# Second layer's causal attention: the output map applied to the values before mixing, one accumulation for all groups

## What is computed

```python
x = x + _L1_attn_ref(_layernorm(x), ...)

def _L1_attn_ref(x, ...):
    q, k, v = split(x @ c_attn_w.T + c_attn_b)      # 3 x 128 features
    q, k, v = heads(q), heads(k), heads(v)          # 16 heads of 8
    q_lat = q @ q2l_w.T + q2l_b                     # 8 -> 32
    k_lat = k @ kv2l_w.T + kv2l_b
    v_lat = v @ kv2l_w.T + kv2l_b
    q_lat = q_lat * cos + _rotate_half(q_lat) * sin
    k_lat = k_lat * cos + _rotate_half(k_lat) * sin
    q_for_k = q_lat @ wqk_w.T + wqk_b
    att = softmax(causal(q_for_k @ k_lat.T * 32 ** -0.5))
    y_lat = att @ v_lat                             # 32 wide
    y = y_lat @ l2o_w.T + l2o_b                     # 32 -> 8, the output map
    return merge(y) @ cproj_w.T + cproj_b
```

## Time and profile before

| | us |
|---|---|
| Median of 3 runs | 4223.95 (4214.59 to 4225.65) |
| The profiled execution's own time | 4192.95 |
| Its span | 4191.1 |
| PE busy / DVE busy / ACT busy / POOL busy | 3748.0 / 2446.0 / 1525.1 / 829.2 |

### The profile page before, as it was taken

One profiled execution on the slowest core, in us unless ns is written; L12 is line 12 of the kernel. 1 busy time (PEld: TensorE's weight loads), 2 busy tenths in 40 slices (PEclk: granted clock), 3 DMA queues, 4 the chain that ended last, 5 costly groups with the idle time before them and its releaser, 6 DMA issues. The chain is left out here.

```text
span 4191.1 us, 95747 instructions
## 1 busy us (share of the span) xinstructions
PE 3748.0 (89%) x38732; PEld 2389.5 (57%) x38732; DVE 2446.0 (58%) x6058; ACT 1525.1 (36%) x3430; POOL 829.2 (20%) x1464
## 2 busy tenths in 40 slices
PE   6998999988898889999979989999788988899999
PEld 3886885433354436665548868854333544366655
DVE  5767675565535466555466777656555344765554
ACT  4445443222222235532244454432222222354322
POOL 1441541010000104220024424400110001033200
PEclk9999999999999999999989999999989999999999
DMA  2000000100000000010010000001000000000100
GB/s 93 3 3 1 3 3 12 41 12 1 21 1 20 1 1 25 1 40 25 5 34 3 3 1 3 3 12 52 1 1 21 1 20 2 12 14 1 40 29 6
DMA packets 8680, 60.05 MB, mean 14 GB/s; under 512 B 893, under 2 KB 5297, under 8 KB 5937
## 3 DMA queue, kind: packets, MB, share of 16 engines
q1 hardware_dynamic: 8240, 53.90, 3.4%
HBM read 52.85 MB, written 1.05 MB: 13 GB/s over the span
## 5 line engine op out<-in xcount | busy, mean ns | idle before, releaser
L97 PE MATMUL psum<-ident_bf 128*128 128x512 bf16 x1528 | 399.3, 393 | 71.6 <-DVE l_attn_peak L930 54.7
L3106 ACT ACTIVATE l_attn_ax<-psum 128x128 f32<-128x128 f32 (+1 forms) x768 | 186.7, 279 | 394.2 <-PE psum L2921 274.8
L3345 DVE TENSOR_TENSOR l_attn_xx<-l_attn_xx,psum 128x256 f32<-128x256 f32 x512 | 205.3, 420 | 209.0 <-PE psum L2940 197.5
L438 ACT ACTIVATE l_ffn_silu<-psum 128x512 f32<-128x512 f32 (+2 forms) x208 | 124.2, 597 | 465.6 <-PE psum L404 411.2
L97 PEld LDWEIGHTS psum<-ident_bf 128*128 128x128 bf16 x1528 | 147.6, 102 | 250.0 <-DVE l_attn_peak L930 69.3
L503 DVE TENSOR_TENSOR l_ffn_hidden<-l_ffn_silu,psum 128x512 f32<-128x512 f32 (+2 forms) x176 | 120.5, 687 | 282.5 <-ACT l_ffn_silu L438 282.4
L103 PEld LDWEIGHTS psum<-streamed_weights,l_ffn_hidden 128*128 128x128 f32 (+2 forms) x1664 | 215.7, 192 | 121.2 <-issue 110.5
L2936 PE MATMUL psum<-l_attn_ax,l_attn_xx 64*64 64x64 f32 x5120 | 269.9, 225 | 0.0
L2940 PE MATMUL psum<-l_attn_xx,l_attn_ax 64*64 64x64 f32 x5120 | 261.9, 221 | 0.0
L3232 POOL TENSOR_TENSOR l_attn_part<-l_attn_ab,streamed_weights 128x128 f32<-128x128 f32 x640 | 245.8, 416 | 39.4 <-PE psum L2921 20.3
L930 DVE TENSOR_REDUCE l_attn_peak<-psum 128x4 f32<-128x2048 f32 (+3 forms) x128 | 186.5, 1488 | 99.4 <-PE psum L822 98.7
(11 more groups left out here) (535 smaller groups left out, 7843.4 us busy)
## 6 DMA issues: line engine op xcount, KB each, us to landing
streamed_weights<-pack_l_ffn SPq DMA_DIRECT2D x2, 5284.0 KB, 15.3
streamed_weights<-pack_l_attn SPq DMA_DIRECT2D x3, 2848.5 KB, 10.2
streamed_weights<-pack_l_ffn SPq DMA_DIRECT2D x2, 3972.0 KB, 12.7
streamed_weights<-pack_l_xattn SPq DMA_DIRECT2D x2, 2496.0 KB, 10.0
streamed_weights<-pack_l_ffn SPq DMA_DIRECT2D x2, 2192.0 KB, 8.3
streamed_weights<-pack_l_xattn SPq DMA_DIRECT2D x2, 2048.0 KB, 7.7
streamed_weights<-pack_l_ffn SPq DMA_DIRECT2D x2, 1923.0 KB, 7.9
streamed_weights<-pack_l_attn SPq DMA_DIRECT2D x2, 1107.5 KB, 5.2
```

The lines of the kernel that those rows point to most:

```text
L97: pe.matmul(self.bank(bank), self.ident_bf[:, :], self.ident_bf[:, :].unsqueeze(1).to_broadcast([P, NT, P]), start=True, stop=True)
L3106: act.activation(ax[b, p, :, :], m.psum[b, p, 0:P].rearrange("p (i t) -> p i t", i=2), ACT.Copy).then_inc(ax_ready, 1)
L3345: dve.tensor_tensor(both, both, m.psum[:, p, P:384], ALU.subtract).then_inc(x_less, 1)
```

## The change

The output map has 8 outputs for every head and is linear, and the softmax weights of a row sum to one, so `att @ v_lat @ l2o.T + b` can be had by mixing values that already went through the map, bias included. The change does that in the preparing block and then calls `causal_attention` as the third layer does.

- The values are made by group, transposed (128 rows of four heads' latents by 512 positions), at n = 1 (two) and n = 3 (two). ScalarE evicts them (`v_latent`).
- At n = 6 four products of 32 columns each apply the output map, into the four quarters of bank 1. ScalarE evicts them with the bias behind its last latent (`vT`); at n = 8 TensorE turns `vT` in four transposes, and ScalarE copies the result into the zeroed, spread-out `v` in four pieces. GpSimd zeroes `v` at the block's start. VectorE's four additions at the end are gone.
- `mixed` has one group, the division is done once, and `early` and the closing block's product and eviction are gone. `cproj`'s rows are reordered on the host.

```diff
-        mixed = sb("mixed", [P, G, T])
+        mixed = sb("mixed", [P, 1, T])
...
+            @block.gpsimd
+            def _(pool):
+                pool.memset(v[:, :, :, :], 0.0).then_inc(v_cleared, 1)
...
-                def values(pe, t):
-                    pe.matmul(m.bank(t), qkv[:, 2, t * P:(t + 1) * P],
-                              w["kv2l"].rearrange("p g c -> p (g c)"), start=True,
-                              stop=True).then_inc(v_psum, 1)
+                def values(g):
+                    if g == 3:
+                        pe.wait_ge(v_latent_ready, 1)
+                    pe.matmul(m.bank(g % 3), w["kv2l"][:, g, :], qkv[:, 2, :], start=True, stop=True).then_inc(v_psum, 1)
...
-                        values(pe, 0)
-                        values(pe, 1)
-                    if n == 2 * G - 1:
-                        values(pe, 2)
+                        values(0)
+                        values(1)
+                    if n == 3:
+                        values(2)
+                        values(3)
+                    if n == 6:
+                        pe.wait_ge(v_latent_ready, G)
+                        for g in range(G):
+                            rows = slice(32 * g, 32 * g + 32)
+                            ins = pe.matmul(m.psum[rows, 1, :], w["l2o"][:, g, rows], v_latent[:, g, :], start=True,
+                                            stop=True, skip_group_check=True)
+                        ins.then_inc(v_out_psum, 1)
                     if n == 2 * G:
-                        values(pe, 3)
+                        pe.wait_ge(vT_ready, 1)
+                        for t in range(NT):
+                            ins = pe.transpose(m.psum[:, 2, t * P:(t + 1) * P], vT[:, t * P:(t + 1) * P], m.ident)
+                        ins.then_inc(v_turned, 1)
...
+                    if 1 <= n <= G:
+                        act.wait_ge(v_psum, n)
+                        act.activation(v_latent[:, n - 1, :], m.bank((n - 1) % 3), ACT.Identity,
+                                       bias=w["kv2l_b"]).then_inc(v_latent_ready, 1)
+                    if n == 2 * G - 1:
+                        act.wait_ge(v_out_psum, 1)
+                        act.activation(vT[:, :], m.bank(1), ACT.Identity, bias=w["l2o_b"]).then_inc(vT_ready, 1)
+                act.wait_ge(v_turned, 1)
+                act.wait_ge(v_cleared, 1)
+                for g in range(G):
+                    act.activation(v[:, :, G * g:G * g + G, HD * g:HD * g + HD],
+                                   m.bank(2).rearrange("p (t q r d) -> p t q r d", t=NT, q=G, d=HD)[:, :, g, :, :], ACT.Copy)
...
-                            tmp = mixed[:, n - G, :]
+                            tmp = turned_k[:, n % 2, :]
...
-                for t in range(NT):
-                    dve.wait_ge(v_psum, t + 1)
-                    dve.tensor_tensor(v[:, t, :, :], m.bank(t).rearrange("p (h l) -> p h l", l=32),
-                                      w["v_b"].unsqueeze(1).to_broadcast([P, H, 32]), ALU.add)
...
-        def early(pe):
-            for g in range(G - 1):
-                pe.matmul(m.bank(0), w["l2o"][:, g, :], mixed[:, g, :], start=g == 0, stop=False)
...
-                         lambda g: m.const["ones"][:, 0:32], False, mixed, early)
+                         lambda g: m.const["ones_of"][:, g, :], True, mixed)
...
-                pe.matmul(m.bank(0), w["l2o"][:, G - 1, :], mixed[:, G - 1, :], start=False, stop=True).then_inc(y_psum, 1)
-                pe.wait_ge(y_ready, 1)
-                m.project(pe, q[:, 0, :], w["cproj"])
-
-            @block.scalar
-            def _(act):
-                act.wait_ge(y_psum, 1)
-                act.activation(q[:, 0, :], m.bank(0), ACT.Identity, bias=w["l2o_b"]).then_inc(y_ready, 1)
+                m.project(pe, mixed[:, 0, :], w["cproj"])
```

More of the change, by code:

```diff
@@ L978, in stage_l1_attn @@
         qkv = psb("qkv", [P, 3, T])
+        v_latent = psb("v_latent", [P, G, T])
+        vT = psb("vT", [P, T])
+        turned_k = psb("turned_k", [P, 2, T])
         LAT, ROT_BANKS = 3, (5, 7)
@@ L990, in stage_l1_attn @@
         v_psum = sem("v_psum")
+        v_latent_ready = sem("v_latent")
+        v_out_psum = sem("v_out_psum")
+        vT_ready = sem("vT")
+        v_turned = sem("v_turned")
+        v_cleared = sem("v_cleared")
         chain_sem = sem("pre_chain")
@@ L1071, in _ @@
                                           ALU.add, ALU.mult).then_inc(wqk_read, 1)
-                for t in range(NT):
-                    dve.wait_ge(v_psum, t + 1)
-                    dve.tensor_tensor(v[:, t, :, :], m.bank(t).rearrange("p (h l) -> p h l", l=32),
-                                      w["v_b"].unsqueeze(1).to_broadcast([P, H, 32]), ALU.add)
         pre.close()
-        def early(pe):
-            for g in range(G - 1):
-                pe.matmul(m.bank(0), w["l2o"][:, g, :], mixed[:, g, :], start=g == 0, stop=False)
         causal_attention(m, name, lambda g: q[:, g, :], lambda g: k[:, g, :], lambda g, r: 4 * g + r, v,
-                         lambda g: m.const["ones"][:, 0:32], False, mixed, early)
-        y_psum = sem("y_psum")
-        y_ready = sem("y_ready")
+                         lambda g: m.const["ones_of"][:, g, :], True, mixed)
         with nc.Block(no_gpsimd_drain=True) as block:
@@ L3780, in pack_l1_attn @@
             ("q2l_b", col(g("q2l_b"), 4)), ("kv2l_b", col(g("kv2l_b"), 4)),
-            ("v_b", np.broadcast_to(g("kv2l_b")[None], (P, 32))), ("wqk", wqk), ("wqk_b", col(g("wqk_b"), 4)),
-            ("l2o", l2o), ("l2o_b", col(g("l2o_b"), 16)), ("cproj", g("cproj_w").T)]
+            ("wqk", wqk), ("wqk_b", col(g("wqk_b"), 4)),
+            ("l2o", l2o), ("l2o_b", col(g("l2o_b"), 16)), ("cproj", g("cproj_w").T.reshape(4, 4, 8, P).transpose(1, 0, 2, 3).reshape(P, P))]
 def pack_l2_attn(i, const):
```

## The result

| | before | changed |
|---|---|---|
| Median of 6 runs each | 4224.17 us (4214.59 to 4225.65) | 4181.95 us (4171.18 to 4194.26) |
| Ratio to before, 95% interval | | 0.9905 (0.9885 to 0.9925) |
| Profiled execution, span | 4191.1 us | 4176.6 us |
| Mean granted clock of the profiled execution | 0.960 | 0.959 |

The two profiled executions, at nearly the same mean clock, are 14.5 us apart. Why the medians say 42 and the profiles 14.5 is what the experiments are about.

A forecast was written before the change was run, and what follows sets the result against it. It took TensorE and VectorE, chained between rotations, to bound the preparing block and exponentials the middle. Stage ends 14.5 us plus preparing blocks 1.0 made 15.5 us off 4223.95: 4208.4 us, range 4195 to 4219.

The forecast's parts named there:

- The end of the stage: Last exponential to projection: without waits for banks and division, output map and eviction, 3.63 us less a stage, 14.5 in four.
- the 30.5 forecast: Preparing block: the scores start 30.5 us after the stage's start, saving 0.5 us per pass, 1.0 in all.
- rival 2: Preparing block grows: the four map products run one after another, 2.7 us more a stage, 4219 us; chance 0.12.
- the change of shape: Output map at n = 6: switching TensorE's tiling twice costs 0.24 us a stage, 1 us in all.
- I count no gain: Pause before the scores, about 2.8 us: no protection against TensorE's clock falling, so no gain counted.
- the 0 of the middle: Mixing in pieces of at most 256 columns costs and saves 0, since the unchanged exponentials set the pace.
- signs of being wrong: Map products in sequence, VectorE waiting for the last rotation, changed exponentials' pace, or first reduction 1.5 us after scores start.
- Rival 1: Clock holds at the scores: stretches match the third layer's, 24.0 us less, 25 us in all, 4199 us; chance 0.14.
- Rival 3: Lower clock falls into worse places: each changed stage loses 1 us more, gain 11.5 us, 4212 us; chance 0.10.
- Rival 4: Slower: new preparing-block waits at n = 6 and n = 8 lower the clock, +57 us net, 4281 us; chance 0.04.

The follow-up runs named there:

- with the pause: Changed kernel with four idle VectorE additions at the preparing block's end, making TensorE's pause before the scores 6.02 us: 4202.77 us, 0.9986 of the kernel before.
- Three shifts: Kernel before with idle VectorE memsets ahead of each pass's first layer, about 1, 2 or 3 us a pass: 4195.48, 4199.18 and 4198.34 us.
- shift 3: Both kernels with the longest idle VectorE memsets ahead of each pass's first layer, 6 us added in all: before 4198.34 us, changed 4197.25 us.
- first comparison: Kernel before and changed kernel, neither with added idle work, six runs each: 4224.17 and 4181.95 us, ratio 0.9905.

## Why the prediction was wrong

**Right in the structure.** The end of the stage is 8.36 us, 3.63 less, in all four. The block is 30.48 us for the 30.5 forecast; VectorE's idle time is 1.99 before the third rotation and 1.10 before the sixth, as forecast; the transposes are done at 975.65, before VectorE's seventh rotation ends at 977.08 (976.39 + 0.69). The map's four products hold the next back by 1.00 us (970.65 to 971.65), so rival 2 is refuted, and the change of shape costs 0.11 rather than 0.24 us above the 0.89 of the earlier trace rows. At the same clock the whole gives 15.9 us.

The Trainium skill, page "TensorEngine Tiling (Array Packing)", section "Key Properties", says that a change of tiling mode drains TensorE; the trace leaves about a tenth of a microsecond for that in the block.

**The step that failed** is "I count no gain" in the part on the clock, together with the 0 of the middle: both treated the clock's losses as a part of the kernel that stays. The 0 rested on the exponentials setting the pace; at the lower level TensorE sets it (the 3.12 us for which an exponential waits above). Two of the prediction's own signs of being wrong came: a first reduction 1.55 us after the scores start, and another pace of the exponentials in a group. The level does not hold through the scores, as predicted, but the conclusion did not follow. The fall came 1.5 us into the scores instead of in the pause, and what counts as much, a later one no longer met the first mixings. In the profiles of before and after that is 26.6 − 14.5 = 12.1 us of the second-layer stretches; of these 6.5 us lie between the first and fourth exponential (from 10.93, 10.93, 10.94 and 10.91 to 9.30 in each stage), 5.6 before the first.

**The medians.** Before's 4224.17 us is a span of about 4222. No clock is on record for these six runs; by the line it was near 0.9496 (0.957 − (4222.3 − 4201.0) / 2880); the changed kernel's six runs have 4180.2 and 0.9583. By this estimate the clock makes 0.0087 x 2880 = 25 us of the 42, structure the other 17. That the mean clock of the changed kernel is higher is measured; that it is so for a reason of the change is shown only for the second-layer stages at this position (with the pause the loss comes back). Three shifts give the kernel before a clock of 0.959 to 0.960 too, and shift 3 takes it from the changed one. So the 27 us beyond the forecast are not the change's own: with 1 to 3 us of idle work a pass the difference was 16.1, 14.8 and 1.1 us. The prediction subtracted from a median that lay high in its own scatter, in the three runs then known as in the first comparison, and its range held only 10 to 13 us for the clock; 4190 to 4224 in unchanged code says it needed twice that.

**The rivals.** Rival 1 had nearly the right size for the stretches, 24.0 us for 26.6 measured (its total, 4199, is 17 us above the time), by luck: the clock did not hold through the scores, and where it was made to, the changed kernel's stages did not gain. The Trainium skill, page "TensorE: Matmul & The Clock Gate", section "Why this matters for your kernels", advises against long idle gaps; the traces agree that the 3.01 us pause itself stays at 1.00 and 6.02 us do not, but the fall within the scores, at busy TensorE, follows 1.5 us behind the shorter one. In the changed kernel at shift 3, where the first block's pause is 3.25 us, it falls in the pause (0.69 in the microsecond before the scores) and the first reduction is at 2.71. Rival 3, the lower clock in worse places, did not happen in the second layer of the first result; at shift 3 it happened in the third. Rival 4's waits at n = 6 and n = 8 cost no clock: the two blocks shown have 1.00.

**Open.** Why a mean clock of 0.950 or 0.960 falls to a run of the same kernel, and why the kernel before scatters over 29 us unshifted and over 5 to 10 shifted (in fewer runs), was not settled; the traces show where the level falls, not what sets the moment.

## What to carry to other kernels

Where the granted clock changes level many times in a run, compare kernels at equal mean clock (span against clock over many runs gives the slope) or over several shifts of a microsecond, before a difference under 1% is put down to an edit. Sum the structure from rows and keep the clock as a term of its own in the range, as wide as the unchanged kernel's scatter. A pause of TensorE can be dear twice, for itself and for the products behind it that meet the lower level: the pause given back cost 12.6 us in the blocks and 13.2 in the stretches of its profile.

## What the runs showed of the hardware

- 0.96 us of idle work a pass made a 4211 us kernel 15.9 us faster (0.9964, 0.9952 to 0.9976).
- The granted clock fell to 0.50 with TensorE busy throughout (868 to 869 us in the changed kernel), 1.5 us behind the end of a pause of about 3.0 us in which it had read 1.00.
- The third layer's stretch, the same code each time, took from 79.10 to 83.12 us at shift 3; the granted clock of the longest was 0.92, of the shortest 0.98.
- What lies ahead of the first changed instruction, the same in both kernels, took 827.08 us at a granted clock of 0.98 and 836.57 at 0.96.
- Four products of 32 columns each into the four quarters, 512 positions wide, held TensorE's next product back by 1.00 us together.
